# Who makes the low half of the pair in the lists of rows: VectorE or GpSimd

## The reference, cut to what matters

```python
tok = x.reshape(-1, d)                               # 8192 x 256
gate = jax.nn.softmax(tok @ Wgate.T, axis=-1)        # 8192 x 8
k_cap = bs // E                                      # 1024
vals, idx = jax.lax.top_k(gate.T, k_cap)             # which tokens, for each expert
idx_flat = idx.T.reshape(-1)
g = _ln(tok[idx_flat], mlp_g, mlp_b).reshape(k_cap, E, d)
y = jnp.einsum('ked,ehd->keh', g, fc1s) + b1s
y = jax.nn.gelu(y, approximate=True)
y = jnp.einsum('keh,edh->ked', y, fc2s) + b2s
tok = tok.at[idx_flat].add((y * w[..., None]).reshape(-1, d))
```

## Time and profile before

| | us |
|---|---|
| median of 3 runs | 2434.58 |
| lowest, highest | 2432.95, 2436.35 |
| time of the profiled execution | 2434.36 |
| its span, first to last instruction | 2432.5 |

### The profile page before, as it was taken

How to read it: one execution, slowest core, us unless ns; L and a number is a source line. 1 busy time by engine, 2 the same in 40 slices (tenths; PEclk the granted TensorE clock), 3 DMA queues, 4 the chain that set the end, 5 groups by cost and what they waited for, 6 DMA issues and landing times. The chain is left out here.

```text
span 2432.5 us, 67113 instructions
## 1 busy us (share of the span) xinstructions
PE 2318.0 (95%) x24912; PEld 2059.8 (85%) x24912; DVE 1909.5 (78%) x3776; ACT 1548.8 (64%) x2983; POOL 1030.9 (42%) x939
## 2 busy tenths in 40 slices
PE   7999999999999899999999999999999818999997
PEld 6888888899999788888888888888888717999996
DVE  8999999667667788888888888888888777666663
ACT  6999998766666456565656565656565554556653
POOL 5888888200000234343434343434343203445544
PEclk9999999999999899999999999999999856999998
DMA  4111110101001000000000000000000022334423
GB/s 146 43 41 41 43 39 25 53 25 32 28 26 33 27 17 15 16 14 17 13 17 13 17 13 17 13 17 13 17 13 17 15 61 71 91 95 87 97 52 35
DMA packets 78720, 89.21 MB, mean 37 GB/s; under 512 B 18480, under 2 KB 72496, under 8 KB 76080
## 3 DMA queue, kind: packets, MB, share of 16 engines
q1 hardware_dynamic: 66352, 71.10, 9.4%
q0 software_dynamic: 12288, 17.05, 4.3%
HBM read 62.42 MB, written 25.69 MB: 36 GB/s over the span
## 5 line engine op out<-in xcount | busy, mean ns | idle before, releaser
L1286 POOL TENSOR_TENSOR a_rq<-a_vq,minus_half 128x8 f32<-128x8 f32 x256 | 417.7, 1641 | 97.5 <-DVE a_vq L1310 97.5
L1230 ACT ACTIVATE a_sq<-a_bqk 128x512 f32<-128x512 f32 x256 | 152.9, 597 | 351.3 <-PE a_bqk L130 348.7
L1281 POOL TENSOR_TENSOR a_rstd<-a_veps,minus_half 128x1 f32<-128x1 f32 x63 | 34.8, 552 | 580.5 <-DVE a_veps L1357 580.5
L128 PE MATMUL a_bqk<-wqk_hi,a_h_lo 128*128 128x512 f32 x512 | 207.7, 406 | 3.5 <-DVE a_h_lo L1326 3.5
L130 PE MATMUL a_bqk<-wqk_hi,a_h_hi 128*128 128x512 f32 x512 | 201.2, 393 | 0.0
L129 PE MATMUL a_bqk<-wqk_lo,a_h_hi 128*128 128x512 f32 x512 | 201.0, 393 | 0.0
L1302 DVE TENSOR_TENSOR a_qk<-a_bqk,a_rq 128x512 f32<-128x512 f32 x256 | 175.9, 687 | 29.6 <-POOL a_rq L1286 29.5
L1956 ACT ACTIVATE e_u<-e_bu,e_b 128x512 f32<-128x512 f32 x128 | 88.3, 690 | 150.1 <-PE e_bu L130 147.7
L1215 ACT COPY a_vs<-a_ba 64x512 f32<-64x512 f32 x256 | 148.8, 581 | 53.5 <-PE a_ba L130 48.8
L2081 DVE TENSOR_TENSOR e_u_lo<-e_u,e_u_hi 128x512 fp32r<-128x512 f32 x128 | 88.4, 691 | 120.4 <-ACT e_u_hi L1961 120.3
L1294 DVE TENSOR_REDUCE a_ss<-a_sq 128x8 f32<-128x512 f32 x256 | 173.9, 679 | 2.6 <-ACT a_sq L1230 1.0
(11 more groups left out here) (334 smaller groups left out, 8036.6 us busy)
## 6 DMA issues: line engine op xcount, KB each, us to landing
a_qk<-gates_of_rows SPq DMA_DIRECT2D x32, 256.0 KB, 4.3
tokens<-a_xs SPq DMA_DIRECT2D x64, 128.0 KB, 1.7
out<-a_xs SPq DMA_DIRECT2D x64, 128.0 KB, 1.7
e_w<-in_fc1s SPq DMA_DIRECT2D x8, 1024.0 KB, 4.8
e_w<-in_fc2s SPq DMA_DIRECT2D x8, 1024.0 KB, 4.8
a_gate<-gates_of_rows SPq DMA_DIRECT2D x122, 64.0 KB, 2.5
X<-in_x SPq DMA_DIRECT2D x56, 128.0 KB, 2.1
wst<-in_qkv_w SPq DMA_DIRECT2D x16, 128.0 KB, 2.5
```

The source lines that it names most:

```text
L128: tensor.matmul(to, w_lo, x_hi, start=start, stop=False)
L1230: nc.scalar.activation(sq[:, n * BK:(n + 1) * BK], b_qk[:, n * BK:(n + 1) * BK], ACT.Square).then_inc(s["sq"], 1)
L1286: nc.gpsimd.tensor_tensor(rq[:, 8 * n:8 * n + 8], vq[:, 8 * n:8 * n + 8], g.mhalf[:, 0:8], ALU.pow).then_inc(s["rq"], 1)
```

## The change

The low half of the pair moves from VectorE's loop to a loop of GpSimd, with the same operands and the same two waits, and VectorE drops them. In that loop GpSimd issues the gathers one by one: gather 0 behind the pair of expert 3, gather 1 behind that of expert 4, up to gather 4 behind the pair of expert 7, and then gathers 5 to 7 behind each other. Before gather 0 it waits, as it did, for the saved probabilities and the rows of expert 0.

```diff
--- before.py
+++ after.py
@@ -1664,15 +1664,27 @@
-            pool.wait_ge(s["saved"], 16)
-            pool.wait_ge(s["rows_out"], 2)
-            pool.sem_inc(s["held"], 1)
-            for h in range(2):
-                for k in range(GT):
-                    c = h * GT + k
-                    nc.gpsimd.indirect_dma_start(
-                        g.xg[h][:, k, :], None, g.tok_dram.rearrange("t p d -> (t p) d"),
-                        bass.IndirectOffsetOnAxis(g.rows[:, 0, c:c + 1], 0)).then_inc(g.gathered[h], 16)
+            def gather(n):
+                if n == 0:
+                    pool.wait_ge(s["saved"], 16)
+                    pool.wait_ge(s["rows_out"], 2)
+                    pool.sem_inc(s["held"], 1)
+                h, k = n // GT, n % GT
+                nc.gpsimd.indirect_dma_start(
+                    g.xg[h][:, k, :], None, g.tok_dram.rearrange("t p d -> (t p) d"),
+                    bass.IndirectOffsetOnAxis(g.rows[:, 0, n:n + 1], 0)).then_inc(g.gathered[h], 16)
+
+            pool.wait_ge(s["tables"], len(parts))
+            for e in range(E):
+                pool.wait_ge(s["hot_lo"], e + 1)
+                if e >= 2:
+                    pool.wait_ge(s["lists"], e - 1)
+                nc.gpsimd.tensor_tensor(pair[:, e % 2, :, 0:RL, :], hot_lo[:, :, :, :], tile_no[:, :, :, :],
+                                        ALU.mult).then_inc(s["pair"], 1)
+                if e >= 3:
+                    gather(e - 3)
+            for n in range(E - 3, 2 * GT):
+                gather(n)
@@ -1796,9 +1808,6 @@
                 if e < E:
                     if e >= 2:
                         dve.wait_ge(s["lists"], e - 1)
-                    dve.wait_ge(s["hot_lo"], e + 1)
-                    nc.vector.tensor_tensor(pair[:, e % 2, :, 0:RL, :], hot_lo[:, :, :, :], tile_no[:, :, :, :],
-                                            ALU.mult).then_inc(s["pair"], 1)
                     for q in range(2):
                         of = slice(q * (NT // 4), (q + 1) * (NT // 4))
```

## The result

The changed kernel takes 2441.86 us (median of 7 runs) against 2433.23 (7 runs of the kernel before beside it). The ratio is 1.0041, 95% interval 1.003 to 1.0052, so 7.3 to 12.7 us more, 10.0 at the ratio itself: slower, by less than the 12.7 us forecast. The forecast was 2447.1, with a range of 2442.0 to 2453.0. It started from the kernel before as it stood then, 2434.58 in the median; the runs taken beside the changed kernel are 1.35 us lower. The median of 2441.86 lies 0.1 us under the low end of the range; the ratio on 2434.58 gives 2444.6, inside it.

What follows compares the result with a forecast made beforehand. VectorE, without gaps in the lists, and behind them the chain to the first expert matmul were taken as bounds. Lists 11.4 us plus late root 1.3 made 12.7 on 2434.36: 2447.1 us, range 2442.0 to 2453.0.

Steps and rivals of the forecast that it cites:

- the pair's own price: On GpSimd in each turn: the 1024-column product takes 2.36 us, extended from f32 rows; bounds 1.9 and 3.0.
- the root: Behind the lists: four gathers precede group 0's root, making it and the first expert matmul 1.3 us late.
- The pair takes hot_hi's place: In the lists: GpSimd's pair and VectorE's hot_hi run one after the other, costing about 1.43 us a turn, 11.4 in all.
- The formula of a turn: Turns 2 to 7: GpSimd starts at 0.77, pair 2.36, then hot_hi's halves 1.0 and 1.14: 5.27 us against 3.85.
- TensorE should wait for the pair in every turn: In the lists, a sign to look for: TensorE, with 3.6 us of work in turns of over 5, waits for the pair.
- the lower bound from L489: On GpSimd: the pair takes at least 1.9 us, scaled from a 512-column operation of 1.046 us with both inputs broadcast.
- That bf16 brings no discount: On GpSimd: bf16 is no cheaper than f32, judged by a bf16 memset of 512 columns taking 0.530 us.
- TensorE's shortest turn: In the lists: 64 matmuls of 3.56 us plus 0.16 make 3.72, so at most 0.8 us could be gained.
- The gathers in the lists: Behind the pairs of turns 3 to 7: gathers 0 to 4 end before the next hot_lo ends, hidden, costing VectorE nothing.
- The first rival: In the lists: five gathers each hold VectorE 0.95 us, making 17.5 us more, or 2451.9; chance 0.07.
- hot_hi and the pair run side by side: In the lists: bf16 pair and hot_hi overlap, GpSimd sets the pace; 3.8 us more in all, 2438.2; chance 0.05.
- The short pair: On GpSimd: the pair takes about 1.05 us, 2.3 us more in all, 2436.7, no change; decides below 1.39; chance 0.06.

Runs made afterwards that it cites:

- bystander: Kernel before, gathers moved as in the change, plus a GpSimd product each turn into a buffer nobody reads; pair stays on VectorE: 2450.1 us, ratio 1.0066.
- half: Changed kernel, but GpSimd makes only the upper half of the tiles' product (512 columns), VectorE the lower: 2439.02 us, ratio 1.002.
- after_psum: Changed kernel with low and high parts of the places copied to PSUM, so hot_lo and hot_hi read one input there: 2433.19 us, ratio 0.9999.
- price: Changed kernel plus four GpSimd products ahead of the lists, 256 and 512 columns in f32 and bf16: 2446.79 us in one execution.
- gathers_alone: Kernel before with only the gathers moved as in the change, the pair staying on VectorE: 2434.95 us, ratio 1.0005.
- two_a_turn: Changed kernel with two gathers behind each of the pairs 3 to 6 and none behind pair 7: 2447.31 us, ratio 1.0046.
- root_first: Changed kernel with gathers 0 to 3 behind pairs 3 to 6 and gathers 4 to 7 behind the root of group 0: 2444.2 us, ratio 1.004.

## Why the prediction was right

Direction, mechanism and place were right. The size was 2.3 us too large, 12.7 forecast against 10.4 in the account: 1.9 of it from the pair's own price, 0.3 from the root.

**The pair takes hot_hi's place: right.** Turns 0 and 1 in the order half, pair, half; turns 2 to 7 with the pair first, by the 0.2 us that the prediction named: the first half there takes 2.99 to 3.00 us, 3.2 expected; in turns 0 and 1 it is the second half, 3.14 at most. The formula of a turn, 0.77 + pair + 1.0 + 1.14, gives 5.03 with the measured pair of 2.12; measured 5.01 to 5.03. bystander, half and after_psum show the cause, by adding it alone, halving it and taking it away. One sign came out otherwise: "TensorE should wait for the pair in every turn". In turns 2 to 7 it waits for the first half of hot_hi, which the pair has held up and which ends 1.1 us after it, for 1.34 to 1.63 us.

**The pair's own price: mis-sized.** The term that was off is "For 1024 that gives 1.272 + 512 x 0.00212 = 2.36 us". The pair took 2.12; 8 x 0.24 = 1.9 us is the whole difference between the 11.4 us forecast for the lists and the 9.45 measured. The rows chosen as nearest in kind were subtractions; the lower bound from L489 (1.9), a product, and they (2.36) enclose the truth; that it lies in the middle of them is chance. That bf16 brings no discount was right (price).

**TensorE's shortest turn: wrong, without effect.** "its own shortest turn is 3.72" added a gap of 0.16 to a duration of 3.56. Neither repeats back to back: 512 matmuls take 27.46 us, 448 more than 64 for 23.90 more, so 3.41 for each further 64. The gain open to a perfect change was about 2.9 us in the lists (27.4 against 30.3), not 0.8; after_psum took it.

**The gathers in the lists: right.** Gathers 0 to 4 are hidden: turns with and without them differ by 0.02 us, and gathers_alone has the turns of the kernel before. The rule of the Trainium skill, SBUF — State Buffer, section "Who interferes with whom", that whoever issues first gets the shared pair for the whole instruction, was not borne out for gathers: by the prediction it gave 17.5 us, measured were 10.4. The first rival falls with it. What two_a_turn adds, that a pair queued behind a gather goes first, was in no forecast.

**The root: right in place, 0.98 against 1.3 us.** The mechanism was right (gathers_alone, root_first). Gather 4 ended 1.9 us behind the pair, not 2.1, and the root needed no 0.19 of issue time.

**The other rivals.** That hot_hi and the pair run side by side is what after_psum made true, and only by moving an operand. The short pair fails on 2.12 us against the 1.39 from which it would decide.

## What to carry to other kernels

Before work is moved from VectorE to GpSimd, ask what both read: here two-input operations of VectorE with both inputs in SBUF and two-input products of GpSimd ran one after the other, while a memset and the short reads of gathers cost VectorE nothing. So moving 0.61 us off VectorE cost it 1.2 us more a turn, and its busy share rose while it did less. One operand in PSUM was enough to part them. And what is issued ahead of a small operation on the critical chain counts in full: four gathers made the root 1 us late, and moving them behind it made the next root late instead.

## What was not expected of the hardware

- A wait for SBUF's read is booked as duration, not as idle time: hot_hi, 1.22 us, reads 3.00, and no bracket names GpSimd.
- VectorE compares bf16 from SBUF with bf16 in PSUM, broadcast, at the same pace as from SBUF alone: 1.21 against 1.22 us for 2048 columns.
- A pair queued behind a running gather came before a hot_hi that by its recorded start began 0.57 us earlier (two_a_turn).
- A two-input operation of 512 columns on GpSimd took 1.04, 1.15 or 1.27 us: a product of a tensor with itself, a product of two, a difference of two. In f32 and bf16 the first of them took the same. Why they differ is left open.
